# Moving the projections of v to other slots of an attention pipeline

## The reference

```
z = layernorm(x)                                   # 512 x 256 for each item
q = z @ w_q                                        # 16 heads of 128
k, v = split(z @ w_kv)                             # 4 groups of 128 each; 4 heads share a group
scores = q @ k.T * 128 ** -0.5, causal
probs = softmax(scores)
ctx = probs @ v
x = x + concat(ctx of 16 heads) @ w_dense
```

## Time and profile before

| | |
|---|---|
| median of 3 runs | 2627.11 us (2623.79 to 2627.64) |
| the profiled execution: its time, its span | 2624.93 us, 2623.1 us |
| busy share of the span: PE, DVE, ACT, POOL | 96%, 82%, 36%, 35% |
| attention in the span | about 825 to 1805 us |
| of it, item 4 (slots 0 to 15) | 1316.94 to 1435.50 us, 118.6 us |

### The profile page before, as it was taken

The page is one execution under the profiler, slowest core; times in us unless marked ns, Lnnn a source line. Parts: engine busy times, 40 slices in busy tenths (PEclk is TensorE's granted clock), DMA queues, the critical chain, the costliest instruction groups (busy, mean ns, idle before and its releaser), DMA issues. The chain is left out here.

```text
span 2623.1 us, 45221 instructions
## 1 busy us (share of the span) xinstructions
PE 2517.4 (96%) x14116; PEld 2300.1 (88%) x14116; DVE 2157.5 (82%) x6164; ACT 943.6 (36%) x2546; POOL 911.7 (35%) x1950
## 2 busy tenths in 40 slices
PE   6999999999996999999999999997999999999998
PEld 6999999999995888888888888886899999999997
DVE  6888888888886888888888888886888888888887
ACT  3111101111103777777777777774211111111100
POOL 4332333333223434343434343334333332332321
PEclk9999999999998999999999999998999999999999
DMA  6000000000002555555545544555100000000000
GB/s 193 9 1 1 1 1 1 1 1 1 1 25 59 81 91 91 89 93 83 89 91 91 86 93 86 91 91 125 45 3 7 9 9 1 9 9 1 9 9 9
DMA packets 378735, 117.25 MB, mean 45 GB/s; under 512 B 338560, under 2 KB 377472, under 8 KB 378496
## 3 DMA queue, kind: packets, MB, share of 16 engines
q1 hardware_dynamic: 378496, 114.36, 22.5%
HBM read 26.24 MB, written 4.19 MB: 12 GB/s over the span
## 5 line engine op out<-in xcount | busy, mean ns | idle before, releaser
L555 PE MATMUL ffn_ring<-ffn_mix_weights,ffn_yT 128*128 128x384 f32 x5760 | 1154.7, 341 | 7.3 <-DVE ffn_mix_weights L790 5.3
L555 PEld LDWEIGHTS ffn_ring<-ffn_mix_weights,ffn_yT 128*128 128x128 f32 x5760 | 1006.8, 189 | 57.8 <-DVE ffn_mix_sums L725 15.8
L727 DVE SCALAR_TENSOR_TENSOR ffn_mix_sums<-ffn_ring,ffn_w,ffn_mix_sums 128x384 f32<-128x384 f32 x896 | 550.3, 614 | 243.3 <-PE ffn_ring L555 226.7
L605 PE MATMUL ffn_ring<-ffn_out_weights,ffn_avT 128*128 128x512 f32 x1536 | 442.3, 399 | 6.2 <-POOL ffn_avT L1028 4.5
L1541 ACT ACTIVATE attn_exponentials<-attn_exponentials,attn_score_neg_max 128x512 f32<-128x512 f32 (+3 forms) x512 | 285.3, 558 | 169.5 <-DVE attn_score_neg_max L1456 169.4
L1608 POOL CAST attn_probsT_long<-attn_turned_long 128x1024 fp32r<-128x1024 f16 (+1 forms) x256 | 233.0, 939 | 249.0 <-DVE attn_probs L1473 247.8
L605 PEld LDWEIGHTS ffn_ring<-ffn_out_weights,ffn_avT 128*128 128x128 f32 x1536 | 282.8, 189 | 36.0 <-POOL ffn_avT L1028 5.7
L1473 DVE SCALAR_TENSOR_TENSOR attn_probs<-attn_exponentials,attn_prob_factor,attn_probs 128x512 f16<-128x512 f32 (+3 forms) x512 | 254.1, 557 | 28.0 <-ACT attn_probs L1550 27.5
L1550 ACT ACTIVATE attn_probs<-attn_exponentials,attn_prob_factor 128x512 f16<-128x512 f32 (+3 forms) x512 | 250.1, 552 | 31.5 <-DMA attn_turned_long<-attn_probs 15.0
L742 DVE SCALAR_TENSOR_TENSOR x<-ffn_ring,ffn_w_out,x 128x256 f32<-128x256 f32 x512 | 246.9, 482 | 12.1 <-PE ffn_ring L605 5.5
L1297 PE MATMUL attn_scores<-attn_kT,attn_qT 128*128 128x512 f32 (+2 forms) x1152 | 243.1, 338 | 3.0 <-DVE attn_qT L1439 1.5
(11 more groups left out here) (149 smaller groups left out, 3268.5 us busy)
## 6 DMA issues: line engine op xcount, KB each, us to landing
ffn_mix_stage<-in_L_ffn_q_proj_dram SPq DMA_DIRECT2D x32, 128.0 KB, 2.5
ffn_mix_stage<-in_L_ffn_k_proj_dram SPq DMA_DIRECT2D x32, 128.0 KB, 2.5
ffn_mix_stage<-in_L_ffn_v_proj_dram SPq DMA_DIRECT2D x32, 128.0 KB, 2.8
ffn_out_stage<-in_L_ffn_o_proj_dram SPq DMA_DIRECT2D x16, 256.0 KB, 3.0
out_dram<-x SPq DMA_DIRECT2D x8, 512.0 KB, 2.9
x<-in_L_attn_x_dram SPq DMA_DIRECT2D x7, 512.0 KB, 8.1
early_stage<-in_L_attn_w_q_dram SPq DMA_DIRECT2D x4, 512.0 KB, 5.3
attn_dense_stage<-in_L_attn_w_dense_dram SPq DMA_DIRECT2D x4, 512.0 KB, 4.7
```

What stands on the lines that cost most here:

```text
L555: last = pe.matmul(bank[:, 0:QKV], yT[:, t % 2, h, k * P:(k + 1) * P], mix_half(e, wh)[:, k], start=(n == 0), stop=(n == 3 * CK - 1))
L605: last = pe.matmul(bank[:], avT[:, t % 2, h], wo[:, g, wh], start=(i == 0), stop=(i == 2))
L727: dve.scalar_tensor_tensor(into, bank[:, 0:QKV], w[:, t, e:e + 1], into, ALU.mult, ALU.add).then_inc(mix_done, 1)
```

## The change

Only the table in `projections` changes. "before" and "after" are the places of v; q, k and z stay. The program numbers the uses from the table, so their order on PE, ACT and DVE, and the bank of each use, follow from it.

| slot | 0 | 1 | 2 | 4 | 5 | 6 | 8 | 9 |
|---|---|---|---|---|---|---|---|---|
| before | C | C | C, E | E | E | E | E | none |
| after | C | C, E | E | none | C, E | none | none | C, E |

```diff
-    extra = {0: {"C": ("v", 0, 0)}, 1: {"C": ("v", 0, 1)}, 2: {"C": ("v", 0, 2), "E": ("v", 0, 3)}, 3: {"C": ("k", 1)},
-             4: {"E": ("v", 1, 0)}, 5: {"E": ("v", 1, 1)}, 6: {"E": ("v", 1, 2)}, 7: {"C": ("k", 2)},
-             8: {"E": ("v", 1, 3)}, 11: {"C": ("k", 3)}}
+    extra = {0: {"C": ("v", 0, 0)}, 1: {"C": ("v", 0, 1), "E": ("v", 0, 2)}, 2: {"E": ("v", 0, 3)}, 3: {"C": ("k", 1)},
+             5: {"C": ("v", 1, 0), "E": ("v", 1, 1)}, 7: {"C": ("k", 2)}, 9: {"C": ("v", 1, 2), "E": ("v", 1, 3)},
+             11: {"C": ("k", 3)}}
     return {"B": ("q", h + 1)} | extra.get(h, {})
```

## The result

The changed kernel takes 2635.19 us in the median of 8 runs against 2627.38 us for the kernel before, also 8 runs: ratio 1.0034, 95% interval 1.0024 to 1.0044. The medians lie 7.8 us apart, and the ratio says about 9 us: it is slower by 8 to 9 us. One execution of the changed kernel was disturbed and took 11158.31 us; the ratio leaves it out, and without it the median is 2634.81. The profiled execution took 2635.58 us, with a span of 2633.7 us (2624.93 and 2623.1 before).

A forecast was written before the change was run, and what follows sets the result against it. Long slots bound by PE, short ones by a DVE and ACT loop: +0.98 an item, 5.9 for items 1 to 6, +1.6 item 7, +0.3 item 0, +1.0 late transfers: +8.8, 2635.9 us; 8-in-10 range 2624 to 2641.

The forecast's parts named there:

- the late transfers: Delays from late transposed transfers reach E's wait in the next slot: +1.0 us, between 0 and 5.
- item 0: First attention item: slots 1 and 2 cancel, DVE and ACT bound its first slots; +0.3 for slots 4 to 9.
- Slots 1 and 2: E in slot 1 waits for q's low half, +0.93; slot 2 loses C, -0.70; together +0.23 an item.
- Slots 4 and 5: Bare slot 4 is 7.01; slot 5 ends at 7.94 with 0.64 of wait at E; together +0.66 an item.
- Slots 6 to 9: Slots 6 and 8 lose E, -1.37; slot 7 +0.17; slot 9 +1.39, to 7.94; together +0.19 an item.
- Slots 10 and 11: The next `split_probs` comes some 0.1 earlier against PE; DVE-bound slot 11 goes from 8.01 to 7.91: -0.10 an item.
- the rival of a later loop: Late landings in slots 4 to 9 cost 1.1 each, v splits lengthen slot 11 by 0.7: 2641 and above; chance 0.08.
- The mechanism: In slots 1, 5, 9 E waits for q's low half to free its bank: 0.1, 0.6, 0.6 us; chance 0.62.
- a wait of `dense` in slot 9: In slot 9 before the change, `dense` waits another 0.4 after the late scores of tile 0; it was to vanish.
- The rival in which the wait doesn't form: q's low half is done before E; odd slots end at 7.17: -0.8 an item, about -5 us, 2622; chance 0.10.
- the one in which it is half as long: E's wait is halved, q's low half 0.3 earlier: +0.4 an item, +3 us, 2630; chance 0.20 (cancelling).
- Item 7: Attention item without layer norm, its slot 9 is 5.92, 0.63 shorter than the others: +1.6.

The follow-up runs named there:

- `one_v_in_5_and_9`: Against the kernel before, slot 5's v goes from place E to C, slot 8's v to place C of slot 9: 2619.22 us, ratio 0.9974.

## Why the prediction was right

The time, its sign and its size held: +8.8 us forecast, a ratio of 1.0034 (some +9 us) measured, and 2635.9 against 2635.19. The steady slots and the wait behind them were right. That the whole came so near is luck in part: two of its terms, the late transfers and item 0, were not right as argued. The two profiled spans differ by 10.6 us: 2.5 in item 0, 6.9 in items 1 to 6, and 1.3 from item 7 to the end of the attention, beside 0.3, 6.9 and 1.6 forecast.

*What bounds the slots.* Right: long slots lost exactly their v (7.69 to 7.01), and the short ones moved with DVE.

*Slots 1 and 2.* +0.23 forecast, 7.24 and 7.70 measured, +0.24 against the earlier trace rows. The experiment with this part alone gives the same lengths.

*Slots 4 and 5.* +0.66 forecast. In item 4 each point lies within 0.05 of the forecast: scores of tile 0 at 4.08 (4.09), place C at 4.37 (4.37), E at 7.11 (7.13), end at 7.90 (7.94). The two distances that were carried over, 2.54 from `split_probs` to the maximum and 3.04 from there to q's low half, measure 2.55 and 3.03.

*Slots 6 to 9.* +0.19 forecast, slots 7.02, 7.19, 7.01 and 7.94; items 1 to 6 lost 1.3 together there beside 1.1 forecast. Slots 10 and 11: -0.1 forecast, 7.91 measured, and DVE's two splits in slot 9 stayed hidden, so the rival of a later loop is out too.

*The mechanism.* That E waits for the bank is shown from both sides: with the wait taken away 10 us go, with the wait moved to a later release 13 us come. (The prediction gives for a wait of `dense` in slot 9, a line that is not among them; the trace of the kernel before has it, with PE idle for 0.16 and its weight loads for 0.31.) The rival in which the wait doesn't form is out; the one in which it is half as long too.

*Late transfers.* Forecast +1.0. Items 1 to 6 grew by 6.9 where the plain slots give 5.9. The changed kernel has long slots of its own, slot 5 of items 2, 5 and 6 (8.28, 8.83, 8.17) and slot 9 of items 3 and 5 (8.18, 8.25), about 2 us in all, and the kernel before has others that go, such as slot 2 of item 5 (8.86, now 7.70). In each of the five a long transposed transfer issued one to three slots before had landed late. The size fits, and by luck: the forecast counted on about one more such wait in eight slots, and ACT has fewer than before, 12 times and 8.9 us beside 14 times and 13.1. That one now costs PE more is argued and not isolated by a run.

*Items 0 and 7.* Item 0 was to cost 0.3 and cost 2.5, 1.6 of it up to the end of slot 3. E in slot 1 waits for q there too and makes ACT's split of the dense weights late (it starts at 853.38, not 851.76), and the earlier E in slot 2 gives that back: slot 3 begins 0.15 later than before. So far the term held, in which the two cancel. What it had at nothing is the clock. Windows of slot 3 of item 0, kernel before:

```profile
863.91:869.50 5.59, 5.59 (x24) 4.62 (x24) 4.45 (x16) 3.93 (x10) 2.33 (x4) 0.85 0.37 69
```

and after:

```profile
864.06:870.97 6.91, 6.91 (x24) 5.81 (x24) 5.03 (x19) 4.78 (x14) 2.71 (x4) 0.65 0.57 107
```

The same 24 matmuls, with PE busy throughout, take 1.3 us more at a mean granted clock of 0.65 instead of 0.85. The other 0.9 came in slots 4 to 15. Item 7 was to cost 1.6; its 16 slots cost 3.4 (slots 5 and 9 are 8.25 and 8.27, both after a late transfer, and slot 15 is 7.45 instead of 6.31), and the stretch behind them to the end of the attention takes 15.8 us instead of 17.9. Why it gave 2.1 back stays open; without that the forecast would have been further off.

## What to carry to other kernels

Filling the idle time of a slot is worth only what the filling's own resources allow: count the uses of each buffer between two readouts, and place in the slot, from the trace, the moment at which the buffer comes free. A third use of two banks within a short slot turned work that should have filled a gap into a longer gap. Ask of a gap not only how long it is but where it lies: the same v in the same slot cost about half its time in front of the instruction that waited, and its full time behind it.

## What was not expected of the hardware

The stretch of the lower clock at the head of the attention moved. The granted clock was 0.50, the lower of its two levels (1.2 GHz), from about 858.8 to 865.4 us in the kernel before and from about 862.0 to 868.7 in the changed one: the stretch is as long, but 4.6 us of it fall into slot 3 of item 0 and not 1.5. In both kernels it begins within a microsecond of the end of PE's wait for the scores of tile 0 in slot 2, which ends 1.6 us later in the changed one. Before:

```profile
859.81 0.58 PE L1333 MATMUL attn_scores<-attn_kT,attn_qT 128*128 128x256 f32 x1 [3.33 <-DVE attn_score_neg_max L1456]
```

```profile
858.80:865.20 6.40, 4.82 (x18) 4.23 (x19) 4.18 (x19) 4.09 (x13) 1.81 (x2) 0.50 0.55 104
```

and after:

```profile
861.41 0.39 PE L1333 MATMUL attn_scores<-attn_kT,attn_qT 128*128 128x256 f32 x1 [4.28 <-DVE attn_score_neg_max L1456]
```

```profile
862.20:868.60 6.40, 5.27 (x15) 4.21 (x14) 5.10 (x17) 4.81 (x15) 1.73 (x3) 0.50 0.57 108
```

That one slot cost 1.3 us, as much as the new wait did in a whole steady item. From the first matmul of the attention to the first `attend` it is 44.1 to 44.2 us in five of the six traces without a second v in slot 1, 44.9 in the sixth (`one_v_in_5_and_9`), and 44.9 to 45.6 in the four traces with it. So the new order lengthens the head, and some of the 1.6 us can be chance.

That the transposed transfers are of two kinds was not expected either: of the 128 long ones most land some 4.0 us after their issue, but 19 in the kernel before and 23 in the changed one after 5.4 to 5.9. 17 of them are the same heads in both. The cause stays open.
